# Low-rank layer and top-2 expert layer: each expert unit is split into its high and low parts in its own step

## What is computed

```python
# first layer
out  = einsum('btc,oc->bto', x, W_base) + b_base
h    = einsum('btc,erc->bter', x, As)
lora = einsum('bter,eor,be->bto', h, Bs, w)
x    = x + out + lora * 2.0
# second layer: 8 experts, each with gate and up 128 x 512 and down 512 x 128
mlp(x, g, u, d) = einsum('bsi,ih->bsh', gelu(x @ g) * (x @ u), d)
w, sel = top_k(softmax(cond), 2)            # two experts per batch
out = sum over the two chosen experts of w[b, e] * mlp(x[b], expert e)
out = out + mlp(x, shared_gate, shared_up, shared_down)
x   = x + out
```

## Time and profile before

| | |
|---|---|
| median of 3 runs | 135.22 us (134.91 to 135.67) |
| profiled execution, its own time | 135.5 us |
| its span in the trace | 133.8 us, 3280 instructions |
| granted clock of TensorE | 1.0 over the span |
| PE busy | 127.2 us, 95% |
| PE weight load busy | 114.2 us, 85% |
| DVE busy | 88.7 us, 66% |
| ACT busy | 70.9 us, 53% |
| POOL busy | 60.2 us, 45% |

### The profile page before, as it was taken

The page is one execution under the profiler, slowest core; times in us unless marked ns, Lnnn a source line. Parts: engine busy times, 40 slices in busy tenths (PEclk is TensorE's granted clock), DMA queues, the critical chain, the costliest instruction groups (busy, mean ns, idle before and its releaser), DMA issues.

```text
span 133.8 us, 3280 instructions
## 1 busy us (share of the span) xinstructions
PE 127.2 (95%) x869; PEld 114.2 (85%) x869; DVE 88.7 (66%) x172; ACT 70.9 (53%) x134; POOL 60.2 (45%) x110
## 2 busy tenths in 40 slices
PE   6899999999999989996999999999999999999991
PEld 6658787878878869995999999999989999989991
DVE  2668978779977888533376658656855686756732
ACT  3432867976876766120466485657554755711110
POOL 5209384497777644632064543554255504610000
DMA  3898878798000185599345686558799940013822
GB/s 51 245 335 290 287 197 300 227 308 247 12 2 0 39 266 170 157 394 409 144 174 218 238 316 240 193 201 313 260 316 322 347 167 0 0 41 121 248 85 61
DMA packets 14526, 26.56 MB, mean 199 GB/s; under 512 B 2225, under 2 KB 7601, under 8 KB 12977
## 3 DMA queue, kind: packets, MB, share of 16 engines
q1 hardware_dynamic: 14192, 26.35, 58.8%
q10 hardware_dynamic: 320, 0.07, 0.2%
HBM read 12.52 MB, written 1.31 MB: 103 GB/s over the span
## 4 chain that ended last, share of the span: by engine, by line
PE 78%; DVEq 6%; DVE 4%; issue 4%; DMA 3%; ACT 2%; SPq 0%; ACTq 0%
PE bank L999 8%; PE bank L1036 7%; PE bank L1035 7%; PE bank L1034 7%; PE bank L946 5%; PE bank L948 5%; PE bank L947 5%; DVEq L232 5%; PE bank L1016 5%; PE bank L1056 4%; PE bank L962 3%; PE bank L1058 3%; PE bank L1057 3%; PE bank L871 3%; PE bank L964 3%
## 5 line engine op out<-in xcount | busy, mean ns | idle before, releaser
L533 ACT ACTIVATE work<-bank 128x512 f32<-128x512 f32 x48 | 28.7, 598 | 43.0 <-PE bank L1036 18.3
L697 DVE TENSOR_TENSOR bank<-bank,work 128x512 f32<-128x512 f32 x40 | 27.9, 697 | 23.2 <-PE bank L1036 12.5
L714 DVE TENSOR_TENSOR hT_lo<-bank,hT_hi 128x512 fp32r<-128x512 f32 x40 | 27.3, 682 | 1.7 <-issue 0.8
L1034 PE MATMUL bank<-xp,wst 128*128 128x256 f32 x96 | 27.2, 284 | 0.0
L1035 PE MATMUL bank<-xp,wst 128*128 128x256 f32 x96 | 27.2, 283 | 0.0
L1036 PE MATMUL bank<-xp,wst 128*128 128x256 f32 x96 | 27.1, 283 | 0.0
L463 POOL TENSOR_TENSOR wstd<-wexd,wstd 128x512 fp32r<-128x512 f32 x12 | 15.5, 1295 | 23.8 <-ACT wstd L575 23.8
L542 ACT CAST hT_hi<-bank 128x512 fp32r<-128x512 f32 x40 | 23.3, 582 | 2.4 <-DVE bank L697 1.3
L1035 PEld LDWEIGHTS bank<-xp,wst 128*128 128x128 f32 x96 | 18.4, 192 | 0.0
L1036 PEld LDWEIGHTS bank<-xp,wst 128*128 128x128 f32 x96 | 18.4, 192 | 0.0
L1034 PEld LDWEIGHTS bank<-xp,wst 128*128 128x128 f32 x96 | 18.4, 192 | 0.0
(11 more groups left out here) (146 smaller groups left out, 212.7 us busy)
## 6 DMA issues: line engine op xcount, KB each, us to landing
wst<-wex SPq DMA_DIRECT2D x12, 1024.0 KB, 5.0
raw_ex<-n_L_cond_skill_gate_dram SPq DMA_DIRECT2D x8, 256.0 KB, 3.3
raw_ex<-in_L_cond_skill_up_dram SPq DMA_DIRECT2D x8, 256.0 KB, 4.2
sst<-n_L_cond_skill_gate_dram SPq DMA_DIRECT2D x8, 256.0 KB, 3.4
sst<-in_L_cond_skill_up_dram SPq DMA_DIRECT2D x8, 256.0 KB, 4.2
xn<-in_x_dram SPq DMA_DIRECT2D x4, 256.0 KB, 4.6
out_dram<-xT SPq DMA_DIRECT2D x4, 256.0 KB, 2.7
sst<-_L_cond_shared_gate_dram SPq DMA_DIRECT2D x1, 256.0 KB, 4.6
```

Of the source, the lines that this page charges most:

```text
L533: act.activation(gelu_sb[q], gate_ps[q][:, :], ACT.Gelu_apprx_tanh).then_inc(gelu_done, 1)
L697: dve.tensor_tensor(up_ps[u][:, :], up_ps[u][:, :], gelu_sb[q], ALU.mult).then_inc(h_done, 1)
L714: dve.tensor_tensor(hT_lo[:, q, :], up_ps[u][:, :], f32(hT_hi[:, q, :]), ALU.subtract).then_inc(lo_done, 1)
L1034: pe.matmul(of_c, w_hi, x_hi, start=True, stop=False)
```

## The change

In the slots, ACT and DVE split a unit in its own step. ACT: gelu of t, in the even unit the down weights, then the high part of t. DVE: product of t, then the reads of batch numbers (even unit) or the sums (odd unit), then the low part of t. The split behind the loop falls away on both engines. No instruction is added or taken away; buffers, semaphores and the programs of PE, POOL and SP stay. Line numbers behind the edit move by up to 4.

```diff
@@ ScalarE, slot(p, j)
                     gelu(t, n)
-                    if not (isinstance(p, int) and p == 0 and n == 0):
-                        split_h_hi(t - 1, 1 - n, (PB + 2 * j + n - 1) % 3)
                     if n == 0:
                         down_hi(p, j, down_at(act, 2 * p))
+                    split_h_hi(t, n, (PB + 2 * j + n) % 3)
@@ ScalarE, behind the loop of slots
-            split_h_hi(LB - 1, 1, (LB - 1) % 3)
@@ VectorE, slot(p, j)
                     gated(t, n, (PB + 2 * j + n) % 3)
-                    if adds or n == 1:
-                        split_h_lo(t - 1, 1 - n, (PB + 2 * j + n - 1) % 3, split_count(t - 1))
                     if adds and n == 0:
                         where = batches_of(p - 1)
                     if adds and n == 1:
                         add_slot(p - 1, (j + 2) % NBUF, where)
+                    split_h_lo(t, n, (PB + 2 * j + n) % 3, split_count(t))
@@ VectorE, behind the loop of slots
             where = batches_of(NP - 1)
-            split_h_lo(LB - 1, 1, (LB - 1) % 3, split_count(LB - 1))
             gated_single(NF)
```

## The result

The changed kernel takes 135.85 us (median of 15 runs, 135.07 to 136.23) against 135.22 us of the kernel before (15 runs). The ratio is 1.0042, with a 95% interval of 1.0026 to 1.0058: slower by some 0.6 us. The forecast was 137.6 us, slower by 2.4. The time lies in the range and on the right side, and the size was off by a factor of four.

A forecast was written before the change was run, and what follows sets the result against it. The prediction took VectorE's queue, with register reads lengthened by weight copies, to make TensorE wait for low parts, about 2.5 us. Entry +1.45, nine slots +2.05 and end -1.13 gave +2.4: 137.6 us, range 135.0 to 140.6.

The forecast's parts named there:

- what bounds the slots: TensorE loses about 2.5 us in the slots, waiting for low parts held up on VectorE's queue by register reads.
- serial chain: Within a unit: product, ScalarE's high part, then VectorE's low part, 1.50 us behind the odd product's start.
- The entry: Slots 0 and 1: the serial hand-over delays product 2 from 68.50 to 70.0, +1.45 us.
- the end: Last low part 1.50 us behind the last product in place of 2.63: -1.13 us.
- The reads did not keep their length: Denies a rival, chance 0.14: nine slots keep r = 1.6, periods of 5.3, 142.4 us.
- The faster case: Rival, chance 0.08: read pairs under 0.62 us let TensorE set the pace throughout, 133.2 us.
- The case of no change: Rival, chance 0.14: pairs shrink to 0.7 us, TensorE's slack swallows the lag, 134.9 to 135.7 us.
- the term of the nine slots: Nine periods beside weight copies, from product 2 on, take 42.9 us in place of 40.85: +2.05 us.
- the new period is 3.7 + r: VectorE's time per slot in us, r being the pair of reads summed; 4.32 where TensorE is slower.
- mechanism of shorter reads: Nine slots: reads move later, out of the copies; r = 0.9 in six slots, 1.4 in three.
- ScalarE's even half as hidden: Even unit: ScalarE's gelu, read, down weights and high part end by 3.9, before the low part at 4.3.

The follow-up runs named there:

- kernels with cut copies: Nine of the twelve expert-weight copies cut to 16 columns, in the kernel before and in the changed one: 133.67 and 132.88 us.
- kernel with the old entry: Changed kernel with slots 0 to 2 in the old order, the changed order from slot 3 on: 135.66 us, ratio 1.0035.
- divided reads: Second of a slot's two reads moved to the odd unit, in the kernel before and in the changed one: 134.22 and 132.82 us.
- old order with its end mended: Kernel before with a slot's second read moved to the odd unit and the last low part ahead of the reads behind the loop: 133.33 us.

## Why the prediction was right and wrong

**Right: what bounds the slots.** The reads and the hand-overs on VectorE's queue limit the slots, not arithmetic. Without reads, or with short ones, TensorE goes at 4.32 us per slot.

**Right: the serial chain and its two ends.** The entry cost 1.31 us on VectorE (forecast 1.45) and the end gave back 1.20 (1.13). The last low part stands 1.43 us behind its product.

**The rivals.** The reads did not keep their length: the pairs fell from 14.0 to 9.3 us, and the kernels with cut copies show why. The faster case did not come about. The case of no change came close. The prediction gave it all that lies within 0.7 us of the kernel before, and +0.63 lies within it; the interval of 15 runs a side does separate it from nothing (1.0026 to 1.0058). Its mechanism is not what the trace shows, though: it wanted pairs of 0.7 us and the entry's lag worked off. The pairs are 1.03 on the mean, and the lag grew by 0.44 over the nine slots. So the path was that of the forecast and the size that of the rival.

**Wrong: the term of the nine slots, +2.05 us, measured +0.44.** The step that failed is "the new period is 3.7 + r". The measured periods sum to 41.29 us and the reads to 9.3, which leaves 32.0 / 9 = 3.56 us. Both hand-overs were rounded up. The odd low part starts at 1.34 (unrolled) to 1.43 us and not 1.50: the high part ends at 1.32 and the low part starts 0.11 behind it, register steps included, where I took 1.35 and 0.15. The even one starts r + 0.88 behind its product (84.93 - 83.17 with two reads of 0.58 and 0.30) and not r + 1.0. Each is a tenth of a microsecond, but a period is paid nine times: 9 x 0.14 = 1.3 us. The other 0.3 us are the reads, 9.3 in place of the 9.6 I had put in (6 x 0.9 + 3 x 1.4). So the mechanism of shorter reads was sized well in sum, with some luck in how it is made up: the pair of slot 1 is 1.49 us and not 0.9, and the last three are 1.38, 1.08 and 1.09 and not 1.4.

**Wrong, at a small price: ScalarE's even half as hidden.** In three of the nine slots the high part ended last, not the reads. There the low part stands r + 0.93 to r + 1.04 behind its product and not r + 0.88, some 0.25 us in all, which is part of the 32.0 us above.

**What the sum hides: entry and slots are coupled.** Adding the entry's 1.45 us in full was no error of the sum, since its reads of 0.9 us presuppose a lag. But it would be wrong to read the term as what a better entry gives. The kernel with the old entry shows it: its nine slots take 0.93 us more. Counted together, the entry is worth about 0.4 us in the trace, and 0.2 us on the clock (135.66 against 135.85, which the intervals don't separate).

**Wrong: what the change is worth at bottom.** I took the period of 3.7 + r as just about even with TensorE's pace at r = 0.6. It is 4.14 us there, under 4.32, so VectorE can work off the entry's lag: with short or divided reads this order is the better of the two, by 0.8 us with cut copies and by 0.5 with divided reads (132.82 against 133.33 for the old order with its end mended). The gain lies at the ends and not in a faster loop: TensorE's loss is smaller by 0.28 us at the first down matmuls in both comparisons, and with cut copies by 0.46 at the last. What made the order slower here was that both reads stood in the one gap, of 1.43 us, in which they don't fit when a copy runs.

Each half of the change by itself cost as much as both (135.74 and 135.88 against 135.85), by different ways. ScalarE's half pays at the entry, is faster in the nine slots and gains almost nothing at the end. VectorE's half pays at the entry and a little in the slots and gains 1.20 at the end, as the whole does; TensorE lost 3.1 us in it, spread over eight waits for low parts. Left open is why a low part that waits for a later high part costs no more in the slots than the full change; no run takes these waits apart.

## What to carry to other kernels

When a chain repeats, measure its constant to the hundredth from whole periods before you multiply it: two hand-overs rounded up by 0.1 us each made 1.3 us of a forecast of 2.4. Look for waits that already exist in a queue and put reads of registers there one at a time: in the changed order two in one gap made the kernel 0.6 us slower than before, and one in each of two gaps made it 2.3 us faster (132.82 against 135.14). And a lag is not a cost until somebody waits for it; here it even went with shorter reads.

## What the runs showed of the hardware

A read of a register from SBUF takes 0.30 us while the DMA engines are idle. Beside copies within SBUF it takes up to 1.07 us in the kernel before, 1.08 in the changed one and 1.16 in the one with the old entry. The kernels with cut copies show it, 22 of 22 reads at 0.297 to 0.324 us. The kernel with both reads behind the even low part shows the same from the other side: there the first read of a slot is short and the second long (0.32 us at 81.24 with the DMA engines idle, 0.94 at 81.97 with a share of 1.04), the reverse of the kernel before. The order in time shows it too. These are the windows of half a microsecond of the changed kernel in which its reads of 83.16 (0.58 us) and 84.15 (0.30 us) stand, with the DMA share in the last column but one:

```profile
83.00:83.50 0.50, 0.50 (x6) 0.50 (x5) 0.50 (x2) 0.04 (x1) 0.00 (x0) 1.00 0.85 344
83.50:84.00 0.50, 0.50 (x6) 0.50 (x5) 0.35 (x1) 0.50 (x2) 0.00 (x0) 1.00 0.51 197
84.00:84.50 0.50, 0.50 (x7) 0.50 (x6) 0.00 (x0) 0.50 (x3) 0.24 (x1) 1.00 0.08 33
```

The Trainium skill, "SBUF — State Buffer", section "SBUF: two separate sides", says that a DMA and an engine's work cannot slow each other, and leaves contention to a shared engine port and to the DMA side's own ports. For these reads of registers the measurement shows a factor of three and more; which port they pass is shown by no run here. By "DMA: Bandwidth & Descriptors" of the Trainium skill, section "Latency and other measured facts", a tensor_load has a floor of about 600 ns; 22 of 22 reads with cut copies took 0.30 to 0.32 us, so the measurement decides against it.
